# A decoder layer: signs dealt anew over the columns of a recurrence, and the last attention group in another order

## The chip, the cores and the metric

One core of one Trainium2 chip. The time is device microseconds from launch to the end of the program. Engines have one in-order queue each: TensorE (PE) multiplies and transposes, VectorE (DVE) and ScalarE (ACT) work element by element, GpSimd (POOL) masks, SyncE (SP) issues DMAs. They meet only through semaphores.

## The reference, cut to what matters

Two sequences of 1024 tokens, 256 wide, all in float32, go through three sublayers, each followed by a layer norm.

```
x = layernorm(x + gated_linear_attention(x))     # 16 heads, dk = 8, dv = 16
x = layernorm(x + cross_attention(x, ctx, idx))  # every token attends to 64 indexed rows out of 64
x = layernorm(x + transformer_block(x))          # causal attention, then a mixture of 8 experts, top 2
```

The gated attention is a recurrence over time: the state of each head is multiplied by a decay and gains the product of a key and a value; a query reads it out; then an RMS norm per head, a gate and a projection. The cross attention picks its 64 context rows by an integer index, with repeats, so its softmax can be computed from how often each of the 64 rows is named: the kernel counts. In the transformer block every token gets a causal attention, an output projection `a = o @ Wo + bo + x`, a layer norm of `a`, routing logits, a softmax over the best two of 8 experts, and those experts' two-layer GELU networks.

## The kernel before, in words

The kernel is written out engine by engine; `nc.Block()` opens a stage with one list of instructions per engine, and all engines meet between stages. A step is released with `then_inc` on a semaphore and awaited by name with `wait_ge`. There is no planner: the order on each engine is the order in the source. Four stages: the front (`front`, to about 212 us of the profile), the cross attention (`cross_blocks`, to 358), the causal attention (`attend`, to 632) and the experts (`moe`).

**The recurrence, in `front`.** The 256 value columns are worked on as 32 columns `jj` (`NJ`), 16 for each sequence, each an array of 128 partitions by 1024 steps. For each column VectorE runs three instructions: `product(jj)` (L521, value times key, in PSUM to `qh`), `state(jj)` (L526, the scan with the decay), `output(jj)` (L531, times the query). Its loop is `state(jj); product(jj + 1); output(jj)`, followed by a side job at some columns. TensorE spreads the values of column `jj + 2` (`values`, L307) two columns ahead, and after each four columns sums over the key dimension (`sums(q)`, L314) and transposes (`turn(q)`, L320). ScalarE copies between the two (`sums_out`, L685) and after them (`tokens`, L688). `qh` has six buffers, so `product(jj)` also waits for the `sums` of the columns that used its buffer.

Side jobs woven into the loop, by their VectorE step: `parts_lo(n)` (L514) makes the low half of a value group after ScalarE's `parts_hi(n)` (L680); `x_lo(k)` (L505) does so for an input block after ScalarE's `x_hi(k)` (L650); `log_sigmoid(1)` (L511); and the RMS norm of the first two blocks of tokens: `out_square(m)` on ScalarE (L830), `out_means(m)` on VectorE (L834), `out_root(m)` on ScalarE (L838), `out_gated(m)` on VectorE (L843 to L847), `out_turn(m)` on TensorE (L114), `out_copy(m)` on ScalarE (L855), and the projection. Both blocks use the same buffer `z` for `og[m]`: `out_square(1)` writes it after `out_copy(0)`, which waits for `out_turn(0)`, which waits for `out_gated(0)`.

**The signs.** To count indices, ScalarE makes 65 arrays `sign(2 * index + bias)` (`signs`, L695) into a ring of six, `RS`; TensorE adds four at a time into two banks (`counts(u)`, L335 and L337). `taken` says how many signs ScalarE has made by the end of each column. `count_at[u]` is the column at which TensorE runs `counts(u)`, the first by whose start the four are due; the sign `n` waits for `counts((n - 6) // 4)`. In each column the signs stand behind ScalarE's other steps.

**The last group, in `attend`.** The attention goes in 8 groups of 4 heads. In each, 10 quads of up to four PSUM banks of scores are made (`quad_scores(k)` in the last group, L1828 to L1834), ScalarE takes their exponentials (`last_exps(k)`, L2024), GpSimd masks the diagonal ones (`triangle`, L1671), and TensorE sums the values with them (`quad_sums`, L1857). Scores of a quad reuse the banks of the quad before it, so they wait for its exponentials. Into the last group the first block's way from attention output to routing weights is woven: `turn_sums`, `divide`, `turn_rows` and copies, `project` (L122, 16 matmuls), `residual` and `means` (L2276 to L2288), `deviation` on ScalarE (the root, L2240), `normed` (L2292, L2296), `turn_normed` (L114), `normed_copy` on ScalarE (L2244) and `rows_hi` on VectorE, `logits` (L2225), `best_two`, `exps`, `weights`. The exponential and the root have different activation tables. `warm(n, bank)` (L1864) issues n matmuls whose result nobody reads.

**The start of `moe`.** TensorE transposes the biases `eb` into bank 0 (L2479), waits for ScalarE's copy of them to `x_bias` (L2524), then starts the first layer of the first expert in banks 0 and 1 (L2439), whose GELU is L2522. ScalarE makes high parts of weights (L2189) from the buffers `x_raw`, VectorE low parts (L2194), after which SP refills `x_raw`. The routing steps of the later blocks use banks 6 and 7 (`RB`).

## Time and profile before

| | us |
|---|---|
| median of 3 runs | 1396.2 (1394.47 to 1398.4) |
| the profiled execution | 1390.58 |
| its span, first to last instruction | 1388.9 |
| TensorE busy | 1291.1, 93% |
| VectorE busy | 978.2, 70% |
| ScalarE busy | 646.8, 47% |
| GpSimd busy | 138.9, 10% |
| mean granted TensorE clock | 0.979 of full speed |

The busy shares are means over four stages that have different limits, so each stage has to be read by itself. An idle time is written in brackets behind the instruction that ended it, with what it waited for.

### The profile page before, as it was taken

The page shows a single profiled execution, that of the slowest core. Times are in us where ns is not written, and L with a number is a line of the kernel's source. Part 1 is how long each engine was busy: PE and PEld are TensorE (multiplying, and loading weights), DVE is VectorE, ACT ScalarE, POOL GpSimd, SP SyncE. Part 2 cuts the span into 40 slices and gives each one's busy share as a digit, 9 for nine tenths or more (in the row PEclk, how much of TensorE's full clock was granted, in tenths as well). Part 3 has the DMA queues.
Part 4 walks back from the last instruction along what each step waited for, and adds up shares of the span by engine and source line. Part 5 has one row for each costly group of instructions (what it writes and reads, how often), then busy time and mean ns, then how long its engine had stood idle before and what let it go on. Part 6 is the DMA issues. An engine that isn't in the chain of part 4 may idle for free.

```text
span 1388.9 us, 18750 instructions
## 1 busy us (share of the span) xinstructions
PE 1291.1 (93%) x7469; PEld 954.1 (69%) x7469; DVE 978.2 (70%) x1409; ACT 646.8 (47%) x946; POOL 138.9 (10%) x217
## 2 busy tenths in 40 slices
PE   8786768999889999999999999999999999999997
PEld 6353437666655555556888888888888888888886
DVE  7998996798788888856666656655655555556566
ACT  5697564436457877775323323232323223233233
POOL 5000002000513433211000000000000000000000
PEclk9998889999989999999999999999999999999999
DMA  4000001002722221213000012110201102010001
GB/s 137 1 1 0 0 1 35 0 1 71 211 82 58 63 61 51 66 31 107 2 15 17 0 36 71 46 39 16 68 16 39 46 16 68 16 38 16 1 16 46
DMA packets 38599, 55.76 MB, mean 40 GB/s; under 512 B 8976, under 2 KB 23744, under 8 KB 38512
## 3 DMA queue, kind: packets, MB, share of 16 engines
q1 hardware_dynamic: 33328, 43.67, 10.6%
q0 software_dynamic: 3648, 10.09, 2.5%
q8 instruction: 59, 0.97, 0.3%
q10 hardware_dynamic: 1536, 0.81, 0.2%
q14 instruction: 28, 0.23, 0.1%
HBM read 43.73 MB, written 10.55 MB: 39 GB/s over the span
## 4 chain that ended last, share of the span: by engine, by line
PE 50%; DVE 3%; ACT 1%; issue 0%; DMA 0%; ACTq 0%; DVEq 0%
PE PS L2439 24%; PE PS L2452 23%; PE PS L122 1%; PE PS L114 0%; PE PS L2465 0%; DMA x_raw<-L_ffn_e_w 0%; PE PS L2225 0%; DVE OT_all L2596 0%; DVE r_st L2279 0%; DVE r_on L2296 0%; DVE x_mid L2589 0%; DVE x_mid L2587 0%; DVE r_on L2276 0%; PE PS L2477 0%; PE PS L2203 0%
## 5 line engine op out<-in xcount | busy, mean ns | idle before, releaser
L2522 ACT ACTIVATE x_g<-PS,x_bias 128x512 f32<-128x512 f32 x256 | 175.8, 687 | 486.8 <-PE PS L2439 486.7
L2439 PE MATMUL PS<-x_h,x_w 128*128 128x512 f32 x1536 | 400.7, 396 | 0.3 <-ACT x_bias L2524 0.3
L2452 PE MATMUL PS<-x_mid,x_w 128*128 128x512 f32 x1488 | 383.8, 393 | 0.0
L2439 PEld LDWEIGHTS PS<-x_h,x_w 128*128 128x128 f32 x1536 | 287.0, 188 | 65.6 <-ACT x_bias L2524 0.5
L2452 PEld LDWEIGHTS PS<-x_mid,x_w 128*128 128x128 f32 x1488 | 279.3, 188 | 64.4
L2587 DVE CAST x_mid<-x_g 128x512 fp32r<-128x512 f32 x256 | 109.2, 427 | 270.0 <-ACT x_g L2522 270.0
L2065 DVE TENSOR_REDUCE a_M<-PS 128x2 f32<-128x1024 f32 (+1 forms) x144 | 170.6, 1222 | 24.0 <-PE PS L1780 17.4
L2589 DVE TENSOR_TENSOR x_mid<-x_g,x_mid 128x512 fp32r<-128x512 f32 x256 | 177.3, 693 | 8.8
L2003 ACT ACTIVATE f_parts<-PS 128x512 f32<-128x512 f32 x224 | 121.1, 599 | 34.7 <-PE PS L1834 28.4
L1857 PE MATMUL PS<-f_parts,aV 128*32 128x256 f32 (+1 forms) x960 | 74.7, 392 | 0.0
L695 ACT ACTIVATE c_hot<-c_idxT,c_cid 128x1024 bf16<-128x1024 bf16 x65 | 70.2, 1139 | 7.5 <-PE PS L335 7.5
L526 DVE TENSOR_TENSOR_SCAN qh<-decay,qh 128x1024 f32<-128x1024 f32 x32 | 73.0, 2281 | 0.0
L2419 POOL DMA_DIRECT2D x_wb<-route_w x31 | 16.7, 539 | 475.9 <-DVE OT_all L2596 453.3
L1834 PE MATMUL PS<-aQ,aK 64*128 64x512 f32 x192 | 51.7, 495 | 2.8 <-ACT V L2024 2.0
L307 PE MATMUL PS<-vparts,g_sel 128*128 128x512 f32 x128 | 40.4, 441 | 12.9 <-DVE qh L521 11.3
L1834 PEld LDWEIGHTS PS<-aQ,aK 64*128 64x128 f32 x192 | 20.3, 186 | 42.9 <-ACT f_parts L2003 27.9
L2596 DVE SCALAR_TENSOR_TENSOR OT_all<-PS,x_bias,x_wb 128x512 f32<-128x512 f32 x62 | 46.2, 745 | 0.0
L1776 PE MATMUL PS<-aK,aQ 64*128 64x512 f32 (+3 forms) x256 | 37.2, 341 | 9.5 <-DVE a_M L2065 6.8
L1671 POOL TENSOR_SCALAR_AFFINE_SELECT f_parts<-f_parts 128x512 f32<-128x512 f32 x45 | 28.6, 636 | 166.3 <-ACT f_parts L2003 142.4
L2194 DVE TENSOR_TENSOR x_w<-x_raw,x_w 128x1024 fp32r<-128x1024 f32 x32 | 39.1, 1228 | 4.0 <-ACT x_w L2189 4.0
L307 PEld LDWEIGHTS PS<-vparts,g_sel 128*128 128x128 f32 x128 | 23.6, 202 | 25.0 <-DVE qh L521 15.6
L521 DVE TENSOR_TENSOR qh<-PS,KT 128x1024 f32<-128x1024 f32 x32 | 38.5, 1203 | 1.4 <-PE PS L314 1.3
(371 smaller groups left out, 1599.2 us busy)
## 6 DMA issues: line engine op xcount, KB each, us to landing
x_raw<-L_ffn_e_w SPq DMA_DIRECT2D x32, 512.0 KB, 3.7
qk_parts<-f_parts SPq DMA_DIRECT2D x16, 512.0 KB, 3.9
x_wb<-route_w POOLq DMA_DIRECT2D x31, 256.0 KB, 3.4
aK<-qk_parts SPq DMA_DIRECT2D x96, 64.0 KB, 2.7
aQ<-qk_parts SPq DMA_DIRECT2D x96, 64.0 KB, 2.5
X<-x SPq DMA_DIRECT2D x4, 512.0 KB, 7.4
out<-X SPq DMA_DIRECT2D x3, 512.0 KB, 2.9
O<-itok_BxSx SPq DMA_DIRECT2D x2, 256.0 KB, 7.8
```

The costliest lines, as they stand in the source:

```text
L307: last = e.matmul(PS[:, 2 * (jj % 2) + half, :], self.sel[:, j, :], vparts[:, u, n % 2, half * BLK:(half + 1) * BLK], start=u == 0, stop=u ...
L526: e.tensor_tensor_scan(qh[:, jj % RQ, :], decay[:, batch(jj // HD)], qh[:, jj % RQ, :], 0.0, ALU.mult, ALU.add).then_inc(s_h, 1)
L695: e.activation(hot[:, n % RS, :], self.idxT[:, :], ACT.Sign, bias=self.cid[:, c:c + 1], scale=2.0).then_inc(s_sg, 1)
L1834: last = e.matmul(bank, K[q][R, s, tile(TB * h if kind == "k0" else kind)], Q[q][R, s, q0:q0 + BLK], start=True, stop=True)
L1857: last = e.matmul(PS[32 * j:32 * j + 32, 7, dst:dst + w], Vs[m % 2][:, kt, j, :], x, start=k in (0, 3) and half == 0, stop=k in (2, NQD - ...
L2003: e.activation(buf[k][:, j, :], PS[:, 4 + b % 3, :], ACT.Exp).then_inc(A.sem, 1)
L2065: e.tensor_reduce(dst, src, AX.X, ALU.max, negate=True).then_inc(VC.sem, 1)
L2439: last = e.matmul(PS[:, f % 2, :], w1[n % 2][u][:, kt, f * P:(f + 1) * P], self.rows(v, k)[:, kt, :], start=m == 0 and kt == 0, stop=m == ...
L2452: last = e.matmul(PS[:, 2 + 2 * (it % 2) + d, :], w2[n % 2][v][:, f, d * P:(d + 1) * P], mid[u][:, f % RM, :], start=f == 0 and m == 0, st ...
L2522: e.activation(g[s % RG][:, :], PS[:, f % 2, :], ACT.Gelu, bias=b1[:, n, f:f + 1]).then_inc(A.sem, 1)
L2587: e.tensor_copy(mid[0][:, f % RM, :], g[s % RG][:, :]).then_inc(V.sem, 1)
L2589: e.tensor_tensor(mid[1][:, f % RM, :], g[s % RG][:, :], mid[0][:, f % RM, :].bitcast(F32), ALU.subtract).then_inc(V.sem, 1)
```

## The change

In `front`: `taken` is dealt anew. By the end of columns 0 to 15 it was 0, 1, 2, 4, 6, 9, 12, 14, 16, 18, 21, 23, 25, 28, 30, 33; it becomes 0, 1, 3, 6, 9, 14, 16, 17, 18, 19, 20, 22, 24, 27, 29, 32, then 33, 35, 37, ... 47 for columns 16 to 23, 50, and the old values from column 25 on. At each fourth column one sign moves between `sums_out` and `tokens`. VectorE's side jobs move: most by half a column, from behind `output(jj)` to behind `state(jj + 1)`; `out_gated(0)` from column 18 to behind `output(19)`, straight before `out_means(1)`; `out_gated(1)` from behind `output(20)` to behind `output(21)`.

In the last group: the projection is in two pieces of eight matmuls with `quad_scores(5)` between them; the two `warm(2)` before the projection and before `turn_normed` go, and two `warm(2)` come around the last `quad_sums`; TensorE runs sums 3 and 4 ahead of scores 6 and 7; `logits` goes behind `quad_sums(7)`, ScalarE's root behind `last_exps(6)`.

In `moe`: the biases are transposed into the first of the banks `RB`, and TensorE does not wait for their copy.

```diff
-        taken = list(itertools.accumulate((0, 1, 1, 2, 2, 3, 3, 2, 2, 2, 3, 2, 2, 3, 2, 3, *[2] * (HD - 1), 1)))
+        taken = list(itertools.accumulate((0, 1, 2, 3, 3, 5, 2, 1, 1, 1, 1, 2, 2, 3, 2, 3, 1, 2, 2, 2, 2, 2, 2, 2, 3, 3, 2, 2, 2, 2, 2, 1)))
...
                     state(jj)
-                    if jj == 23:
+                    if jj == 2:
+                        parts_lo(1)
+                    elif jj == 6:
+                        x_lo(3, 4)
+                    elif jj == 11:
+                        log_sigmoid(1)
+                    elif jj == 12:
+                        parts_lo(2)
+                    elif jj == 18:
+                        self.out_means(e, 0)
+                    elif jj == 19:
+                        parts_lo(3)
+                    elif jj == 23:
                         self.out_rstd(e, 0)
...
                     output(jj)
-                    if jj == 1:
-                        parts_lo(1)
-                    elif jj == 3:
+                    if jj == 3:
                         x_lo(2, 4)
-                    elif jj == 5:
-                        x_lo(3, 4)
-                    elif jj == 10:
-                        log_sigmoid(1)
-                    elif jj == 11:
-                        parts_lo(2)
-                    elif jj == 17:
-                        self.out_means(e, 0)
-                    elif jj == 18:
-                        parts_lo(3)
+                    elif jj == 19:
                         self.out_gated(e, 0)
-                    elif jj == 19:
                         self.out_means(e, 1)
-                    elif jj == 20:
+                    elif jj == 21:
                         self.out_gated(e, 1)
...
                         sums_out(jj // 4 - 1)
+
+                        signs(range(taken[jj - 1], taken[jj - 1] + 1))
                         tokens(jj // 4 - 1)
...
-                    signs(range(taken[jj - 1] if jj else 0, taken[jj]))
+                    signs(range(taken[jj - 1] + (jj % 4 == 0) if jj else 0, taken[jj]))
...
                 quad_sums(NG - 1, 2)
-                warm(2, SPARE)
-                self.project(e, 0, FREE)
-                for k in range(5, 8):
+                self.project(e, 0, FREE, range(2))
+                quad_scores(5)
+                self.project(e, 0, FREE, range(2, TB))
+                for k in range(6, 8):
+                    quad_sums(NG - 1, k - 3)
                     quad_scores(k)
-                    quad_sums(NG - 1, k - 2)
-                warm(2, SPARE)
+                quad_sums(NG - 1, 5)
+                quad_sums(NG - 1, 6)
                 self.turn_normed(e, 0, FREE)
-                quad_sums(NG - 1, 6)
                 quad_scores(8)
+                quad_sums(NG - 1, 7)
                 self.logits(e, 0, FREE)
-                quad_sums(NG - 1, 7)
                 quad_scores(9)
                 quad_sums(NG - 1, 8)
+                warm(2, SPARE)
                 quad_sums(NG - 1, 9)
+                warm(2, SPARE)
...
                 last_exps(5)
+                last_exps(6)
                 self.deviation(e, 0)
-                last_exps(6)
...
-                e.transpose(PS[:, 0, 0:E * (NF + KD)], self.eb[:, :], self.ident[0:E * (NF + KD), 0:E * (NF + KD)]).then_inc(SM.sem, 1)
-                e.wait_ge(A.sem, A.at("b1"))
+                e.transpose(PS[:, RB[0], 0:E * (NF + KD)], self.eb[:, :], self.ident[0:E * (NF + KD), 0:E * (NF + KD)]).then_inc(SM.sem, 1)
```

## Rows read from the trace of the kernel before

**Rows 1.** Windows, two stretches: busy us (instructions) by engine, clock, DMA, GB/s.

```profile
24.00:200.00 176.00, 129.57 (x729) 80.48 (x728) 165.15 (x136) 120.94 (x128) 0.00 (x0) 0.89 0.00 1
590.00:632.80 42.80, 37.33 (x334) 22.02 (x330) 22.70 (x49) 31.05 (x56) 8.36 (x12) 0.96 0.09 26
```

**Rows 2.** Timeline, VectorE, recurrence: start, us, instruction, [idle before it, released by].

```profile
35.89 1.22 DVE L514 TENSOR_TENSOR vparts<-PS,vparts 128x1024 fp32r<-128x1024 f32 x1 [1.85 <-ACT vparts L680]
...
56.72 1.23 DVE L505 TENSOR_TENSOR XTp<-PS,XTp 128x1024 fp32r<-128x1024 f32 x1 [0.68 <-ACT XTp L650]
...
87.36 1.22 DVE L514 TENSOR_TENSOR vparts<-PS,vparts 128x1024 fp32r<-128x1024 f32 x1 [1.48 <-ACT vparts L680]
...
117.42 1.22 DVE L834 TENSOR_REDUCE go_ms<-z 128x64 f32<-128x1024 f32 x1 [2.15 <-ACT z L830]
...
139.29 0.55 DVE L843 RECIPROCAL go_rs<-go_rs 128x64 f32<-128x64 f32 x1 [1.97 <-ACT go_rs L838]
...
193.23 2.48 DVE L601 TENSOR_TENSOR c_Kblk<-PS,c_m 128x512 f32<-128x512 f32 x4 [0.43 <-PE PS L465]
...
200.52 0.69 DVE L984 CAST vparts<-PS 128x512 fp32r<-128x512 f32 x1 [0.69 <-PE PS L114]
```

**Rows 3.** Timeline, VectorE: one scan and the product behind it.

```profile
142.28 2.28 DVE L526 TENSOR_TENSOR_SCAN qh<-decay,qh 128x1024 f32<-128x1024 f32 x1
144.48 1.20 DVE L521 TENSOR_TENSOR qh<-PS,KT 128x1024 f32<-128x1024 f32 x1
```

**Rows 4.** Timelines of VectorE, TensorE, ScalarE: from `out_gated(0)` to `out_square(1)`.

```profile
126.07 1.23 DVE L847 TENSOR_TENSOR z<-z,G 128x1024 f32<-128x1024 f32 x1
...
127.44 1.94 PE L114 MATMUL PS<-ident,z 128*128 128x128 f32 x8 [4.24 <-DVE z L847]
...
129.42 1.02 ACT L855 ACTIVATE QT<-PS 128x1024 f32<-128x1024 f32 x1 [3.15 <-PE PS L114]
130.34 1.05 ACT L830 ACTIVATE z<-O 128x1024 f32<-128x1024 f32 x1
```

**Rows 5.** Timeline, ScalarE, recurrence: a gate copy, `tokens(0)`, the two signs of column 28.

```profile
40.34 1.03 ACT L675 ACTIVATE G<-PS 128x1024 f32<-128x1024 f32 x1 [3.45 <-PE PS L283]
...
52.69 1.05 ACT L688 ACTIVATE O<-PS 128x512 f32<-128x512 f32 x1 [1.18 <-PE PS L320]
...
188.97 2.16 ACT L695 ACTIVATE c_hot<-c_idxT,c_cid 128x1024 bf16<-128x1024 bf16 x2
```

**Rows 6.** Timeline, TensorE, last group: projection, scores 5, logits.

```profile
607.79 3.61 PE L122 MATMUL PS<-r_Wo,r_onT 128*128 128x256 f32 x16
611.33 0.73 PE L1834 MATMUL PS<-aQ,aK 64*128 64x512 f32 x4
...
625.31 1.95 PE L2225 MATMUL PS<-r_Wr,r_onT 128*128 128x8 f32 x16
```

**Rows 7.** Timeline, ScalarE, last group: exponentials 5, root's table, exponentials 6, 8.

```profile
611.93 2.06 ACT L2024 ACTIVATE V<-PS 128x512 f32<-128x512 f32 x4 [2.81 <-PE PS L1834]
614.01 1.28 ACT L2240 ACT_TABLE_LOAD   x1
...
616.92 2.07 ACT L2024 ACTIVATE V<-PS 128x512 f32<-128x512 f32 x4
...
625.19 2.06 ACT L2024 ACTIVATE f_parts<-PS 128x512 f32<-128x512 f32 x4 [0.71 <-PE PS L1829]
```

**Rows 8.** Windows, TensorE alone: busy (instructions), granted clock, DMA, GB/s.

```profile
604.00:608.00 4.00, 4.00 (x39) 1.00 0.01 2
...
616.00:618.00 2.00, 0.43 (x1) 1.00 0.00 0
...
620.00:622.00 2.00, 2.00 (x15) 0.50 0.00 0
```

**Rows 9.** Timeline, TensorE: the first layer's first six matmuls in `moe`.

```profile
633.43 2.87 PE L2439 MATMUL PS<-x_h,x_w 128*128 128x512 f32 x6 [0.33 <-ACT x_bias L2524]
```

**Rows 10.** The chain that ended last, in order of time: start, us, what.

```profile
645.48 5.29 DMA x_raw<-L_ffn_e_w
```

More of the change, by code:

```diff
@@ L2209, in turn_rows, with project @@
         self.transposes(e, self.on, 0, rb).then_inc(self.SR.sem, 1)
-    def project(self, e, m, rb):
-        e.wait_ge(self.VR.sem, self.VR.at("onT0", m))
-        e.wait_ge(self.AR.sem, self.AR.at("onT1", m))
-        self.token_major(e, self.onT, self.Wo, rb).then_inc(self.SR.sem, 1)
+    def project(self, e, m, rb, ts=range(TB)):
+        if 0 in ts:
+            e.wait_ge(self.VR.sem, self.VR.at("onT0", m))
+            e.wait_ge(self.AR.sem, self.AR.at("onT1", m))
+        last = self.token_major(e, self.onT, self.Wo, rb, ts)
+        if TB - 1 in ts:
+            last.then_inc(self.SR.sem, 1)
     def turn_normed(self, e, m, rb):
@@ L2523, in _ @@
                 e.wait_ge(SM.sem, SM.at("b1"))
-                e.activation(bias[:, :], PS[:, 0, 0:E * (NF + KD)], ACT.Copy).then_inc(A.sem, 1)
+                e.activation(bias[:, :], PS[:, RB[0], 0:E * (NF + KD)], ACT.Copy).then_inc(A.sem, 1)
                 for q in range(2, 4):
```

## The prediction

> **What bounds the kernel now.** I read the windows by stage first, then the timeline of the engine that is fullest in each changed stage, then the chain of waits. In the recurrence, 24 to 200 us, VectorE is busy 165.2 of 176 us and no other engine is as full [rows 1]. So the time of this stage is VectorE's work plus its stalls, and the reader is to look for the brackets: 1.85 and 1.48 before two `parts_lo`, 0.68 before `x_lo(3)`, 2.15 before `out_means(0)`, 1.97 before `out_gated(1)`, 0.43 before the key blocks, 0.69 at the stage's end [rows 2]. The last group, up to 632.8, is different: TensorE is busy 37.3 of 42.8, ScalarE 31.1, VectorE 22.7 [rows 1], so a loop through several engines sets its end: scores on TensorE, exponentials on ScalarE, and once each the root and the normed rows. There the reader is to see ScalarE idle 2.81 us for scores 5, which stood behind the whole projection [rows 6, 7]. In `moe` TensorE is nearly full, so what comes before it is passed on whole: the stages are separated by a meeting of all engines, and no transfer that started in an earlier stage is late in the next.
>
> **The recurrence.** The work of VectorE is the same, instruction for instruction; only stalls change. Removed are 1.85 + 0.68 + 1.48 + 2.15 + 1.97 = 8.1 us [rows 2], if each awaited step is now done in time. One scan, 2.20 us from start to start [rows 3], goes between.
> - `parts_lo(1)`: VectorE was free at 34.0, one scan later it is 36.2, and ScalarE's high part was there at 35.9. No stall.
> - `x_lo(2)` is not moved, but gets early. Behind 36.2 come `parts_lo(1)` and four multiplications at 1.12 each and a scan: 44.0. ScalarE's gate copy, at 40.34 before [rows 5], follows `parts_lo(1)` and starts at 40.6; then two signs instead of one, at 1.08 each (2.16 for two [rows 5]), and `x_hi(2)`, 1.0: 44.8. A new stall, 0.8.
> - `x_lo(3)`: its high part was ready at 56.7 [rows 2]. It now comes 1.15 earlier by what is gained so far, but sign 6 stands before `tokens(0)` and waits for `counts(0)`, which TensorE runs behind its turn: 1.0 for the counts and 1.1 for the sign, so 57.6. VectorE is there at 57.0. New stall 0.6. At the other fourth columns the sign placed there is not held up, and fits into the 1.18 us that ScalarE idles before `tokens` [rows 5]; it costs nothing and takes 1.08 off what stood behind.
> - `parts_lo(2)` is wanted at 86.6 and ready at 85.2: fewer signs in columns 7 to 10 bring ScalarE's steps forward.
> - `out_means(0)` is wanted at 114.45. The copy before the square moves up with ScalarE and the square ends near 113.7: no stall. `parts_lo(3)` is wanted at 120.04, ready at 119.97; cover is gone if ScalarE is 0.1 later, and costs what it is late.
> - `out_means(1)` is the price. It now follows `out_gated(0)` directly, and waits for `out_square(1)`, which writes the same buffer and so waits for that very gate. Before, the gate ended at 127.3 (126.07 + 1.23) and the square at 131.4 (130.34 + 1.05) [rows 4]: transposes 1.94 at the low clock, copy, square and the hand-overs, 4.1 us. Before, column 19's scan and multiplications lay beside it. Now nothing does: a new stall of 4.1. Queued behind it on VectorE is the state of column 20, and all that follows.
> - `out_gated(1)` comes a column and a half later than the root it waited 1.97 for: free. Its own work is 142.28 - 139.29 = 3.0 us [rows 2, 3], unchanged.
>
> In the loop 8.1 - 0.8 - 0.6 - 4.1 = 2.6 us go; a stalled instruction also loses the 0.08 by which the next else overlaps [rows 3], two stalls fewer, 0.2: 2.8. At the end, the sign in the gap before `tokens(6)` frees ScalarE 0.8 sooner for the copies of the context keys, whose follower stalled 0.43, and for the last six signs, on which TensorE's last counts and transposes hang, which stalled VectorE 0.69 [rows 2]. I take 0.7 of the 1.1. The stall before `product(30)` depends on the second block's norm and stays. Sum: 3.5 us. Bounds: no gain but the tail's (0.7), if `parts_lo(3)`, `x_lo` and `out_means(1)` eat the rest; and 4.5, if the transposes run at the full clock and the x stalls vanish.
>
> **The last group.** TensorE is through with sums 2 at 607.2. Half of the projection (3.61 / 2 [rows 6]) brings it to 609.0, where scores 5 begin instead of at 611.33. ScalarE starts 0.60 behind them (611.93 - 611.33 [rows 6, 7]): 609.6, 2.3 earlier; its table, buffers and the copy before it are ready. The second half ends at 611.5 and the residual starts as before. The mean and variance are there at 614.7 as before. Sums 3 (1.07 us) then stand before scores 6, so ScalarE's exponentials 6 run 613.1 to 615.1. The root with its two table loads takes 614.01 to 616.92, 2.9 us [rows 7]; it now runs 615.1 to 618.0, and exponentials 7 end at 620.1. That is only 0.8 ahead of before (620.9). The normed rows are ready at 618.35, 1.0 later than before, but TensorE turns them at once, being through with sums 5 and 6 at 617.3, and not behind scores 7, a sum and a warm-up. So the copy of them follows exponentials 7 directly (620.1, 0.8 us) and exponentials 8 run from 620.9 instead of 625.19 [rows 7]: 4.3 earlier. Behind these: sums 7 wait for the mask (620.8) and end at 621.9, logits 1.95 us [rows 6] to 623.8, scores 9, exponentials 9 from 624.4 to 625.5 (before 628.8), mask, sums 9, copy, as before. The end of the stage keeps the 4.3 to 4.4. The warm-ups around sums 9 lie beside the mask and the last copy and cost nothing, within 0.2. I take 4.3. Upper bound 5; lower 2.5, if TensorE is at half clock from 618.4 on: then turn, scores 8, sums 7 and logits take 1.8 us more.
>
> **The start of `moe`.** TensorE no longer idles 0.33 [rows 9]. But the first GELU is followed by weights that ScalarE takes from `x_raw`, and the chain goes through the landing of these (5.29 us [rows 10]); they are issued by work that starts at the copy of the biases, which does not move. So most of it is lost there. I take 0.1; bounds 0 and 1.1: at the full clock the six matmuls would take 1.4 instead of 2.87 [rows 9].
>
> **Sum.** 3.5 + 4.3 + 0.1 = 7.9 us. The profiled execution took 1390.58, so its like would take 1382.7. The median of the runs is 5.6 above that execution, and I take the difference off it: 1396.2 - 7.9 = 1388.3.
>
> **Rivals.** A measurement of this kernel can tell about 0.3%, 4.2 us, from no change.
> - A, the clock takes part of the last group. After 616 to 618 with TensorE busy 0.43 of 2 us, the granted clock was 0.50 in 620 to 622, the 1.2 GHz level [rows 8]. The new order still has a wait of about 1.0 at 617.3, and two warm-ups are gone. The group then gives 2.5: total 6.1, 1390.1. For it: the wait. Against: it is half as long, and before it TensorE works from 607 on.
> - B, the recurrence gives only its tail: the stall at `out_means(1)` grows or `parts_lo(3)` is late. Total 0.7 + 4.3 = 5.0: 1391.2. For it: the margin of 0.07 us.
> - C, what is gained in the last group is hidden anyway: if the weights for `moe`, or the low clock at its start, set the pace, the gain there is absorbed. About 3.5 at most is left: 1392.7, and with B, 1395.5. Against: the first weights landed long before, and later loads are issued by work of the stage itself.
> - D, slower. The warm-up at 607.2 and the next were what kept TensorE at 2.4 GHz; without them it falls to 1.2 GHz from the projection on. About 17 us of TensorE's work lie from there to the end of the group, nearly all on its path. Each us of it at the low level costs another; past 7.8 us of it, the whole gain is gone. With all 17: 17 - 7.8 = 9 slower, 1405; with 12: 1400. Against: TensorE hardly pauses there; four us before, also full of transposes, have clock 1.00 [rows 8].
>
> The Trainium skill, "TensorE: Matmul & The Clock Gate", Part 4: PE-mode transpose, says that transposes do not count as TensorE activity for the clock in the same way as matmuls. It would speak for A and D, since two warm-ups leave a stretch with turns in it. By that rule D's time would be 1400 to 1405. The window 604 to 608, a quarter of it transposes, has the full clock, so the trace does not bear the rule out here.
>
> **Chances.** Forecast 0.62, A 0.15, B 0.08, C 0.10, D 0.05. The forecast's own range is 1386 to 1391. The range to hold 8 in 10 takes in A and B, the upper bounds of the terms (1396.2 - 4.5 - 5 - 1.1 = 1385.6), and about 1.5 us of scatter in a median: 1384.5 to 1393.5. Faster by over 0.3%, below 1392.0: forecast, A, most of B, 0.82. Within 0.3%: C and the rest of B, 0.13. Slower: D, 0.05.
>
> **What would show it.** Right: VectorE's bracket before `out_means(1)` near 4.1 and none before `out_means(0)`, `out_gated(1)` and the `parts_lo`; brackets of 0.8 and 0.6 before `x_lo`; the second stage 3.5 earlier; exponentials 5 at 2.3 earlier and 8 at 4.3 earlier against the group's start; TensorE's clock 1.00 in the group. Wrong: a clock below 1 between 607 and 618 (D) or after it (A), a `parts_lo(3)` with a stall over 1 us (B), or a new wait for `x_raw` in `moe` as long as what was gained (C).

## The result, and the profile after

| | before | after |
|---|---|---|
| median, us | 1396.45 (6 runs, 1391.48 to 1398.4) | 1388.34 (6 runs, 1382.51 to 1391.79) |
| ratio | | 0.9941, 95% interval 0.9918 to 0.9964 |
| the profiled execution | 1390.58 | 1391.79 |
| its span | 1388.9 | 1390.1 |
| its mean granted TensorE clock | 0.979 | 0.975 |

The change takes 0.6% off, and the interval excludes both no change and the 0.3% that a measurement can just tell. 1388.3 had been forecast. Twelve kernels were measured later, in three groups of four, each group beside the kernel before on one chip; the changed kernel, measured again among them, had 1388.40 and a ratio of 0.9951 (0.9931 to 0.997).

But the two profiled executions say the opposite: after is 1.2 us longer than before. That of before was shorter than all six times in its median, that of after was the longest of its six. The first thing to look at is the clock. The changed kernel was profiled a second time ("after, again"): there its span was 1381.6 us at a mean granted clock of 0.983, and the first time 1390.1 us at 0.975. 8.5 us lie between two executions of one program. Over all 68 later runs of the kernel before, the time falls by about 0.93 us for each 0.001 of mean granted clock; over those of the changed kernel by 1.1 to 1.2. So below, a kernel has two figures: its ratio to before, and its time at equal clock, read off a line through its own runs at clock 0.979 (their scatter about the line is 0.4 to 1.2 us). By the line before has 1390.9 and after 1387.2: 3.7 us less. The rest of the 8.1 goes with the median clock, 0.975 before and 0.9785 after. The line is an aid to reading and no price: where a kernel has more of the full clock because its path has changed, the reading at equal clock takes that part from the change. It is also uncertain: the lines of single kernels, of 6 to 12 runs, have slopes from 0.5 to 1.5 us per 0.001, and 0.979 is the upper end of what before ever had. With one slope for all kernels, 0.97, the readings are 1390.8 for before and 1387.3 for after, so these two stand; where another reading hangs on the slope, both are given below.

The shares of the changed kernel (page, first part: busy us, share, instructions) show no less work. VectorE and ScalarE are as busy as they were, and TensorE is busy longer, because part of its work ran slower:

```profile
PE 1296.3 (93%) x7469; PEld 958.2 (69%) x7469; DVE 977.2 (70%) x1409; ACT 647.5 (47%) x946; POOL 139.2 (10%) x217
```

**The recurrence after.** VectorE's stalls of the loop and its tail, timeline of the changed kernel:

```profile
46.48 1.23 DVE L505 TENSOR_TENSOR XTp<-PS,XTp 128x1024 fp32r<-128x1024 f32 x1 [2.06 <-ACT XTp L650]
60.57 1.22 DVE L505 TENSOR_TENSOR XTp<-PS,XTp 128x1024 fp32r<-128x1024 f32 x1 [1.78 <-ACT XTp L650]
89.91 1.23 DVE L514 TENSOR_TENSOR vparts<-PS,vparts 128x1024 fp32r<-128x1024 f32 x1 [0.28 <-ACT vparts L680]
118.35 1.22 DVE L836 TENSOR_REDUCE go_ms<-z 128x64 f32<-128x1024 f32 x1 [0.51 <-ACT z L832]
134.61 1.22 DVE L836 TENSOR_REDUCE go_ms<-z 128x64 f32<-128x1024 f32 x1 [4.13 <-ACT z L832]
...
192.33 1.23 DVE L521 TENSOR_TENSOR qh<-PS,KT 128x1024 f32<-128x1024 f32 x1 [1.17 <-PE PS L307]
...
202.42 0.69 DVE L986 CAST vparts<-PS 128x512 fp32r<-128x512 f32 x1 [0.82 <-PE PS L114]
```

As [rows 2] are read, the brackets of 1.85 and 1.97 are gone, 1.48 has become 0.28 and 2.15 has become 0.51. In their place stand 4.13 before `out_means(1)` and 2.06 and 1.78 before the two `x_lo`. Together 8.8 us, where 8.1 had stood: in this execution the loop gained nothing. A wait of 1.17 before the last product is new beside them. TensorE's work ahead of that product ran at the low clock: the eight transposes of `turn` took 1.97 us, and in the second execution 1.09, without the wait.

```profile
187.62 1.97 PE L320 MATMUL PS<-ident,OT 128*128 128x128 f32 x8 [1.14 <-ACT OT L685]
```

The second execution of the same program:

```profile
45.33 1.22 DVE L505 TENSOR_TENSOR XTp<-PS,XTp 128x1024 fp32r<-128x1024 f32 x1 [0.57 <-ACT XTp L650]
121.50 1.23 DVE L514 TENSOR_TENSOR vparts<-PS,vparts 128x1024 fp32r<-128x1024 f32 x1 [1.50 <-ACT vparts L680]
132.09 1.22 DVE L836 TENSOR_REDUCE go_ms<-z 128x64 f32<-128x1024 f32 x1 [4.12 <-ACT z L832]
...
197.79 0.69 DVE L986 CAST vparts<-PS 128x512 fp32r<-128x512 f32 x1 [0.45 <-PE PS L114]
```

Here only 6.2 us of stall are left in the loop, and the stage is through 4.6 us sooner. The 4.12 does not vary; the others do. The transposes inside the 4.12 stand behind a long pause of TensorE, and took 1.94 us in all 14 profiles. For the others, look at TensorE's gate matmuls, which ScalarE and then `x_lo(2)` wait for. In the first execution, then in the second:

```profile
37.77 4.63 PE L283 MATMUL PS<-Wgp,XTp 128*128 128x256 f32 x24 [1.77 <-DVE vparts L514]
```

```profile
38.11 3.14 PE L283 MATMUL PS<-Wgp,XTp 128*128 128x256 f32 x24 [1.77 <-DVE vparts L514]
```

The same 24 matmuls after the same wait of 1.77 us take 1.5 us more, and the stall of `x_lo(2)` is 1.5 longer. Over 24 to 212 us the granted clock was 0.88 in the first and 0.91 in the second (before: 0.90).

**The last group after**, where it ran at full clock, that is in the second execution. TensorE, with line 1836 the scores of quad 5, 114 the turn of the normed rows, 1859 sums 9, 1866 the second warm-up, 2487 the first matmul of `moe`:

```profile
606.65 0.73 PE L1836 MATMUL PS<-aQ,aK 64*128 64x512 f32 x4
...
616.19 1.09 PE L114 MATMUL PS<-ident,r_on 128*128 128x128 f32 x8 [0.88 <-DVE r_on L2304]
...
623.96 0.64 PE L1859 MATMUL PS<-f_h,aV 128*32 128x256 f32 x8 [0.26 <-POOL f_h L1673]
624.52 0.73 PE L1866 MATMUL PS<-a_idr 128*128 128x512 f32 x2
626.17 0.26 PE L2487 MATMUL PS<-ident,r_eb 80*128 80x80 f32 x1 [0.91 <-PEq L1636]
```

and ScalarE beside it (exponentials 5, the root's table, exponentials 8):

```profile
607.25 2.06 ACT L2029 ACTIVATE V<-PS 128x512 f32<-128x512 f32 x4 [0.63 <-PE PS L1836]
...
612.91 1.28 ACT L2248 ACT_TABLE_LOAD   x1
...
618.40 2.09 ACT L2029 ACTIVATE f_parts<-PS 128x512 f32<-128x512 f32 x4
```

The group's first scores began at 588.28 here and at 590.76 before. From there: scores 5 come 18.37 us in, where it was 20.57 (611.33, [rows 6]); exponentials 8 come 30.12 in, where it was 34.43 (625.19, [rows 7]); the group takes 37.89, where it took 42.08. The 2.81 us of ScalarE's idling [rows 7] is 0.63. TensorE's windows have clock 1.00 throughout (busy, instructions, clock, DMA share, GB/s):

```profile
590.00:600.00 10.00, 9.59 (x97) 1.00 0.32 96
600.00:612.00 12.00, 12.00 (x106) 1.00 0.03 11
612.00:626.00 14.00, 11.91 (x116) 1.00 0.00 1
```

In the execution of after that was profiled first, the group took 40.12 us, and TensorE was at its 1.2 GHz level twice:

```profile
598.00:600.00 2.00, 2.00 (x16) 0.51 0.00 0
600.00:602.00 2.00, 2.00 (x24) 0.64 0.03 8
...
628.00:630.00 2.00, 2.00 (x18) 0.69 0.00 0
630.00:632.00 2.00, 2.00 (x14) 0.50 0.04 8
```

**The start of `moe`.** Its first six matmuls took 1.62 us instead of 2.87 [rows 9], but the gain is mostly waited away: TensorE, the changed kernel.

```profile
634.39 0.26 PE L2487 MATMUL PS<-ident,r_eb 80*128 80x80 f32 x1 [1.01 <-PEq L1636]
634.54 1.62 PE L2447 MATMUL PS<-x_h,x_w 128*128 128x512 f32 x6
...
638.88 3.00 PE L2447 MATMUL PS<-x_h,x_w 128*128 128x512 f32 x12 [0.88 <-ACT x_g L2529]
```

ScalarE still waits for the landing of `x_raw`, in the second execution:

```profile
632.43 1.06 ACT L2194 ACTIVATE x_w<-x_raw 128x1024 fp32r<-128x1024 f32 x1 [0.80 <-DMA x_raw<-L_ffn_e_w]
```

From the first matmul of `moe` to that of the kernel's last group of matmuls it is 742.24 us before, 741.89 and 741.64 in the two executions of after. Over all profiles this length is 741.49 to 742.24 with the old start (five, mean 741.91) and 741.25 to 742.37 with the new one (nine, mean 741.82).

### The profile page after: what moved, and what is told of

Read it like the earlier page. It is cut to its first block, busy times and chain, and to the rows that moved or that the text cites. A ratio compares the mean times of both kernels' runs of the same rounds, so it can differ in the third digit from the quotient of the medians.

```text
span 1390.1 us, 18750 instructions
## 1 busy us (share of the span) xinstructions
PE 1296.3 (93%) x7469; PEld 958.2 (69%) x7469; DVE 977.2 (70%) x1409; ACT 647.5 (47%) x946; POOL 139.2 (10%) x217
## 4 chain that ended last, share of the span: by engine, by line
PE 50%; DVE 3%; DMA 1%; issue 0%; ACT 0%; ACTq 0%; DVEq 0%
PE PS L2447 24%; PE PS L2460 23%; PE PS L122 1%; DMA x_raw<-L_ffn_e_w 1%; PE PS L114 0%; PE PS L2473 0%; PE PS L2233 0%; DVE x_w L2199 0%; DVE OT_all L2603 0%; DVE r_st L2287 0%; DVE r_on L2304 0%; DVE x_mid L2596 0%; DVE x_mid L2594 0%; DVE r_on L2284 0%; PE PS L2485 0%
## 5 line engine op out<-in xcount | busy, mean ns | idle before, releaser
L307 PEld LDWEIGHTS PS<-vparts,g_sel 128*128 128x128 f32 x128 | 24.5, 209 | 21.4 <-DVE qh L521 10.5
```

Of the source, the lines that this page charges most:

```text
L307: last = e.matmul(PS[:, 2 * (jj % 2) + half, :], self.sel[:, j, :], vparts[:, u, n % 2, half * BLK:(half + 1) * BLK], start=u == 0, stop=u ...
```

## The experiments

Each is a kernel of its own. "At clock 0.979" is the reading described above. Each ratio is to runs of before on the same chip; experiments 1 to 4, 5 to 8 and 9 to 12 had one chip each, so medians are compared only within these groups.

**1 to 3: the parts alone, and the whole again.** Front only: the new `taken` and VectorE's new order, nothing else.

```diff
-        taken = list(itertools.accumulate((0, 1, 1, 2, 2, 3, 3, 2, 2, ...
+        taken = list(itertools.accumulate((0, 1, 2, 3, 3, 5, 2, 1, 1, ...
...
                     state(jj)
+                    if jj == 2:
+                        parts_lo(1)
```

> The change of the front stage alone (signs and VectorE order), last group and experts as before. Theory 1 (each part brings its own stalls' worth, as forecast): VectorE's idle time in the recurrence falls by 2.6 to 3.5 us and the median by 3.5, ratio 0.9975. Theory 2 (the one profile of after read literally: the front stage ends 1.9 us later than before): the median rises by about 2, ratio 1.0014, and the whole gain of the change comes from elsewhere. A profile with new stalls of 0.8 and 0.6 before the two x_lo speaks for 1, one with about 2 each for 2.

Last group only:

```diff
-                self.project(e, 0, FREE)
+                self.project(e, 0, FREE, range(2))
+                quad_scores(5)
+                self.project(e, 0, FREE, range(2, TB))
...
-                self.deviation(e, 0)
                 last_exps(6)
+                self.deviation(e, 0)
```

> The new order of the last attention group alone. Theory 1: the group ends 4.3 us earlier, ratio 0.9969; from the first scores of the group to the first matmul of the experts 37.8 us instead of 42.1. Theory 2 (as the one profile of after shows, where this stretch took 40.1): 2.0 earlier, ratio 0.9986, because TensorE ran at the low clock at the end of the group and the two matmuls put before sums 9 then delay them.

The changed kernel again, with no edit:

> The changed kernel unchanged, for a second profile and more times. Theory 1 (the change is worth about 8 us, and the first profile was taken in an execution with more low clock): ratio 0.994, and at a mean clock of 0.978 or more the profile shows the front stage ending earlier than 212.4 us, as the kernel before does. Theory 2 (front stage slower by itself): the front ends after 213.5 again.

| | median us | ratio (95%) | at clock 0.979 |
|---|---|---|---|
| front only | 1392.58 | 0.9986 (0.9974, 0.9998) | 1388.3 |
| last group only | 1390.89 | 0.9978 (0.9964, 0.9993) | 1389.3 |
| after, again | 1388.40 | 0.9951 (0.9931, 0.997) | 1387.2 |

The front is worth 2.0 us by its ratio (0.3 to 3.6) and 2.6 at equal clock (1.6 with the common slope), the last group 3.1 (1.0 to 5.0) and 1.6 (1.8). The last group's own length, first scores to the first matmul of `moe`: 40.13 with the last group only, 43.86 with the front only, both with stretches at the low clock, against 37.89 (after, again) and 42.08 (before). Like is to be compared with like here. In six of the 14 profiles TensorE's clock fell some five us into the group, before anything that the change moves, and the steps behind it came 1.0 later. Without this fall the old order takes 42.08 to 42.24 (four profiles) and the new one 37.89 to 37.98 (four): 4.2 less. With it, the old order takes 43.86 (one) and the new one, as in the changed kernel, 40.12 to 40.16 (three): 3.7 less. With the group's old order the clock fell behind TensorE's pause before the turn, as in [rows 8]; windows of the front only:

```profile
620.00:622.00 2.00, 2.00 (x8) 0.50 0.00 0
```

The front's stalls in its own profile (VectorE from 24 to 204 us: who waited for whom, us in total, times, longest):

```profile
DVE go_ms L836 <- ACT z L832: 4.5, 2, 4.1
...
DVE XTp L505 <- ACT XTp L650: 1.3, 2, 0.7
...
DVE vparts L514 <- ACT vparts L680: 0.9, 2, 0.6
```

The `x_lo` stalls add to 1.3, near the forecast's 0.8 and 0.6, and the means stand for 4.1.

**4: the forecast's price taken back.** `out_means(1)` goes one column later, so that the scan and the multiplications of column 20 lie beside the transposes, the copy and the square.

```diff
                     elif jj == 19:
                         self.out_gated(e, 0)
+                    elif jj == 20:
                         self.out_means(e, 1)
```

> The changed kernel with the means of the second block (out_means(1)) one column later, behind output(20). In after VectorE idles 4.1 us for the square that this step needs, directly behind the gate that the square waits for. Theory 1: that stall is a pure loss; with a column of 4.45 us between, it goes whole and the root and gate of block 1 are still in time: 4 us faster than after, ratio to before 0.991. Rival: the root, which stands on ScalarE behind tokens(4), is then late, the gate behind output(21) stalls 1 to 2 us, or product(22) waits for sums(4): 1 to 2 us are left of the 4.

Measured: 1382.34 (1377.85 to 1387.31), ratio 0.9915 (0.9892 to 0.9938); at clock 0.979, 1383.1. Its stalls (VectorE, as above):

```profile
DVE XTp L505 <- ACT XTp L651: 1.3, 2, 0.8
...
DVE go_ms L837 <- ACT z L833: 0.6, 1, 0.6
```

The 4.1 is gone and nothing took its place; the 0.6 is that before `out_means(0)`. In medians the kernel is 6.1 us faster than the changed one beside it, by the ratios 5.0, at equal clock 4.1, the stall itself. It does not rest on this one kernel: the four with this edit (4, 5, 6, 12) read 1382.7 to 1383.5 at equal clock, and the changed kernel and its two neighbours without it (10, 11) 1386.9 to 1387.2. The kernel has the lowest median of all, and beats both kernels.

**5: without the warm-ups around sums 9**, on top of experiment 4.

```diff
-                warm(2, SPARE)
                 quad_sums(NG - 1, 9)
-                warm(2, SPARE)
```

> r4_means_later without the four warm-up matmuls around sums 9. In two of three profiles with the new group TensorE was at the low clock there, and the two before sums 9 then delayed them by 0.9 us. Theory 1 (the warm-ups cost where the clock is low and buy nothing, since the first GELU of the experts waits for weights from x_raw anyway): 0.5 us faster than r4_means_later in the median, and the first matmuls of the experts may be at the low clock without moving anything behind them. Theory 2 (they keep the clock up into the experts, which counts): 1 to 1.5 us slower than r4_means_later, the first six matmuls of the experts in 2.9 instead of 1.6 us and their end passed on.

Measured: 1383.41, ratio 0.9911 (0.9894 to 0.9929), at clock 0.979 1382.7. Not to be told from experiment 4. The clock fell at the logits in its profile too (the sums behind them took 1.93 us, the 1.2 GHz level), and the warm-ups then no longer stood before sums 9.

**6: `x_lo(2)` half a column later**, on top of experiment 4.

```diff
                     state(jj)
+                    elif jj == 4:
+                        x_lo(2, 4)
...
-                    if jj == 3:
-                        x_lo(2, 4)
```

> r4_means_later with x_lo(2) behind state(4) instead of behind output(3), a scan later. Theory 1: its stall (0.6 to 0.8 us with TensorE at the full clock before it, 2.06 with the low clock) goes wholly or to 0, and nothing else is late: 0.7 us faster than r4_means_later at the full clock, up to 2 at the low one, and less scatter. Rival: sums(0) wait for this step on TensorE, so turn(0), the sign and x_lo(3) get 1 to 2 us later: the stall moves there and the sum is 0.

Measured: 1385.15, ratio 0.9926 (0.9904 to 0.9949), at clock 0.979 1383.5: no gain. The stall moved:

```profile
58.79 1.23 DVE L505 TENSOR_TENSOR XTp<-PS,XTp 128x1024 fp32r<-128x1024 f32 x1 [2.62 <-ACT XTp L651]
```

`x_lo(2)` has no bracket any more, and `x_lo(3)` has 2.62. TensorE's `sums(0)` start only behind `x_lo(2)`, and the whole way from there to `x_lo(3)` hangs on them: from one `x_lo` to the other it is 12.7 us here and 13.1 in experiment 4, so a later `x_lo(2)` makes `x_lo(3)` late. The 2.62 is not to be set against the 0.57 and 0.75 of experiment 4, whose gate matmuls took 3.14 us. Here they took 4.63, as in the first profile of after, where the two brackets add to 3.8.

**7 and 8: the front's two parts apart.** Signs only: the new `taken` and the sign before `tokens`, VectorE's order as before. Order only: the opposite.

```diff
+                        signs(range(taken[jj - 1], taken[jj - 1] + 1))
                         tokens(jj // 4 - 1)
```

> The kernel before with the new deal of signs alone; VectorE's order, last group and experts as before. Theory 1 (signs make ScalarE's steps of columns 7 to 19 earlier, and VectorE's order turns that into fewer stalls; alone each is worth little): without the order, the waits for parts_lo(1) (1.85) and gated(1) (1.97) stay, x_lo(2) and x_lo(3) gain 1 to 2 us of stall, parts_lo(2) and means(0) lose 1 to 2: within 1 us of before. Theory 2 (the deal is the part that pays): 2 us faster.

```diff
                     state(jj)
+                    elif jj == 18:
+                        self.out_means(e, 0)
...
+                    elif jj == 19:
+                        self.out_gated(e, 0)
+                        self.out_means(e, 1)
```

> The kernel before with VectorE's new order of side jobs alone, old deal of signs. Theory 1: the stalls before parts_lo(1), x_lo(3), parts_lo(2) and gated(1) go (6.0 us), means(0) loses most of its 2.15, the 4.1 before means(1) comes, parts_lo(3) may be 1 to 3 late: 2 to 3 us faster than before, so the order is what pays in the front. Theory 2 (the order needs the signs): ScalarE is late at parts_lo(2), means(0) and parts_lo(3), within 1 us of before.

| | median us | ratio (95%) | at clock 0.979 |
|---|---|---|---|
| signs only | 1391.18 | 0.9976 (0.9956, 0.9997) | 1389.7 |
| order only | 1395.47 | 1.0005 (0.9993, 1.0017) | 1393.7 |

The signs alone save 3.3 us (0.4 to 6.1), the order alone none. At equal clock it would cost 2.8 by its own line, whose slope of 0.5 is the flattest of all, and 1.2 with the common slope; by its ratio it is between 1.0 better and 2.4 worse. The stalls with the signs alone:

```profile
DVE vparts L514 <- ACT vparts L680: 1.8, 1, 1.8
DVE XTp L505 <- ACT XTp L650: 1.3, 1, 1.3
...
DVE go_rs L844 <- ACT go_rs L839: 0.9, 1, 0.9
```

Of the five brackets in [rows 2], those before `out_means(0)` and `parts_lo(2)` have gone with nothing moved on VectorE, and 1.97 is 0.9. (This profile had a clock of 0.94 over 24 to 212 us, the others 0.86 to 0.91.) With the order alone:

```profile
DVE go_ms L834 <- ACT z L830: 5.4, 2, 4.1
DVE z L511 <- ACT decay L666: 2.0, 1, 2.0
...
DVE vparts L514 <- ACT vparts L680: 1.5, 1, 1.5
DVE XTp L505 <- ACT XTp L650: 1.3, 1, 1.3
```

the 4.1 is there, and a 2.0 before `log_sigmoid(1)`, which before's profile has not; but experiment 2, with nothing moved in the front, had 1.3 there.

**9: `moe` only.** ScalarE's copy of the biases reads the new bank too.

```diff
-                e.transpose(PS[:, 0, 0:E * (NF + KD)], ...
-                e.wait_ge(A.sem, A.at("b1"))
+                e.transpose(PS[:, RB[0], 0:E * (NF + KD)], ...
```

> The kernel before with the new start of the experts alone (biases transposed into another bank, TensorE not waiting for their copy). Theory 1: the stage is set by the landing of x_raw, so of the 0.33 us 0.1 to 0.35 are left: not to be told from no change in the median; in the profile, from the bias transpose to the last matmul group 741.9 us instead of 742.2. Theory 2 (more, if the low clock at the stage's start is shortened as well): 1 us.

Measured: 1394.62, ratio 0.9991 (0.9981 to 1.0001), at clock 0.979 1391.1 (before 1390.9). The rest of the kernel behind the transposes took 741.92 in its profile, 742.24 before. That is 0.3 less, within what such a length varies by.

**10: the two removed warm-ups back**, in the changed kernel.

```diff
                 quad_sums(NG - 1, 2)
+                warm(2, SPARE)
                 self.project(e, 0, FREE, range(2))
...
                 quad_sums(NG - 1, 6)
+                warm(2, SPARE)
                 self.turn_normed(e, 0, FREE)
```

> The changed kernel with the two removed warm-up pairs back, ahead of the projection and ahead of turn_normed. Theory 1 (the clock does not need them there): the first pair adds its 0.6 to 0.7 us to the chain, as scores 5 stand behind it, the second lies in the wait for the normed rows and costs 0: 0.6 us slower than the changed kernel. Theory 2 (rival D of the prediction, without them the clock falls in the group): 2 us faster than the changed kernel, with the share of the low clock smaller in the group.

Measured: 1390.59, ratio 0.9960 (0.9943 to 0.9977); at clock 0.979, 1386.9 against 1387.2. By the ratios 1.3 us slower than after, again, within the intervals, at equal clock the same; this is not settled. What it does show: in this execution the warm-ups did not hold the clock. The second pair ran at 620.56, and behind it TensorE's windows show:

```profile
624.00:626.00 2.00, 2.00 (x26) 1.00 0.00 0
626.00:628.00 2.00, 2.00 (x17) 0.67 0.00 0
628.00:630.00 2.00, 2.00 (x17) 0.50 0.04 8
```

**11: the changed kernel with VectorE's old order.**

```diff
                     output(jj)
+                    if jj == 1:
+                        parts_lo(1)
...
-                        self.out_means(e, 1)
-                    elif jj == 21:
+                    elif jj == 19:
+                        self.out_means(e, 1)
+                    elif jj == 20:
                         self.out_gated(e, 1)
```

> The changed kernel with VectorE's order of before in the recurrence: new signs, new last group, new start of the experts. Signs alone gave 3.8 us, the order alone nothing, both 2.6. Theory 1 (with the new signs, the order costs more by its 4.1 us before means(1) than it saves at parts_lo(1), x_lo(3) and gated(1)): 0 to 2 us faster than the changed kernel, ratio to before 0.993 to 0.994. Theory 2 (the parts add as single medians say only by chance; at an equal clock both together were 1.4 us better than signs alone): 1 to 1.5 us slower than the changed kernel.

Measured: 1385.92 (8 runs, 1380.58 to 1393.16), ratio 0.9943 (0.9921 to 0.9966), at clock 0.979 1387.2, as after. So the order brought nothing that can be measured, also when all the rest is there. It may pay once its 4.1 is removed: experiment 4, which differs from this kernel in VectorE's order alone, reads 1383.1 at equal clock, but by the ratios, 0.9915 and 0.9943, the two are not clear of each other. The profile has one stall of 4.8 us in the place of the 4.1 (VectorE, 24 to 204 us):

```profile
DVE XTp L505 <- ACT XTp L650: 4.8, 1, 4.8
```

It belongs to this execution: the same front had 1.3 there in experiment 7. TensorE, ahead of it, was at the low clock here (transposes 1.97 us, there 1.09):

```profile
52.37 1.97 PE L320 MATMUL PS<-ident,OT 128*128 128x128 f32 x8 [1.14 <-ACT OT L685]
```

**12: sign 6 behind `tokens(0)`**, on top of experiment 4.

```diff
                         sums_out(jj // 4 - 1)
-                        signs(range(taken[jj - 1], taken[jj - 1] + 1))
+                        if jj > 4:
+                            signs(range(taken[jj - 1], taken[jj - 1] + 1))
                         tokens(jj // 4 - 1)
...
-                    signs(range(taken[jj - 1] + (jj % 4 == 0) if jj else 0, taken[jj]))
+                    signs(range(taken[jj - 1] + (jj > 4 and jj % 4 == 0) if jj else 0, taken[jj]))
```

> r4_means_later with sign 6 behind tokens(0) instead of before. There it waits for counts(0), which TensorE runs behind its turn, and holds tokens(0) and with it x_hi(3). Theory 1: tokens(0) comes 2 to 4 us earlier, the stall before x_lo(3) (0.75 us in r4_means_later's profile, 1.8 in after's) goes, 0.7 to 1.5 us faster than r4_means_later. Rival: the three signs then stand before x_hi(3), or x_hi(3) waits for TensorE's transposes all the same: no change.

Measured: 1383.78, ratio 0.9910 (0.9893 to 0.9927), at clock 0.979 1383.2: as experiment 4. ScalarE in its profile:

```profile
53.85 1.05 ACT L689 ACTIVATE O<-PS 128x512 f32<-128x512 f32 x1 [2.06 <-PE PS L320]
55.69 3.23 ACT L696 ACTIVATE c_hot<-c_idxT,c_cid 128x1024 bf16<-128x1024 bf16 x3 [0.78 <-PE PS L337]
```

`tokens(0)` went first, and then the signs waited for `counts(0)` all the same. The bracket before `x_lo(3)` is 0.74. In experiment 4 it was 0.75, but there TensorE's transposes ahead of it took 1.09 us, and here 1.97. The first profile of after had 1.97 too, and a bracket of 1.78; against it ScalarE's `x_hi(3)` now starts at 58.82 instead of 59.53. So where the clock is low the edit may save up to 1 us; the times do not show it.

## Why the prediction was right, and where its steps were not

**The sum.** 7.9 us forecast, 8.1 by the first medians, 6.8 by the ratio of the second set (4.2 to 9.6). The first is the forecast; the second lies between it and A. That the median came within 0.1 us of 1388.3 is luck: the single times of after lie 9.3 us apart. Added up by the lengths of the stages, the parts make 4.2 + 2.6 + 0.1 = 6.9; by the ratios of the parts alone it is 2.0 + 3.1 + 1.3 = 6.4, the 1.3 of `moe` being not clear of nothing; read at equal clock the whole makes 3.7. These don't agree, and what of the 8.1 is path and what clock stays open.

**The last group, 4.3: right.** Scores 5 2.2 us earlier (forecast 2.3), exponentials 8 4.3 earlier (4.3), the group 4.2 shorter (4.3), where the clock stayed up in its first part and again behind the logits. Rival C did not happen: `moe` keeps its length, so what the group gains is passed on. The steps between hold too: the root followed exponentials 6 with two table loads at 1.28, and the turn waited 0.88 (about 1.0 forecast).

Rival A is a part of the truth. In the first profile the low clock took 1.0 at 598 to 602, before anything that the change moves, and the rest at the end. The group is 2.0 shorter there than in before's profile, near A's 2.5, but that one had no early fall; against the old order with such a fall, experiment 1, it is 3.7 shorter. And A's place was wrong: the clock was 1.00 around the wait at the turn (616 to 626 in both profiles of after), and fell from the logits on.

"The warm-ups around sums 9 cost nothing" failed where the clock is low. At full clock the mask ended the wait before sums 9 (0.26, the row at 623.96). In the first profile sums 9 started at 632.06, directly behind the warm-up; by the distance between the exponentials 9 and their mask in the second execution (623.96 less 622.11, 1.85) it could have started at 631.05. That is 1.0 us, outside the 0.2 that was given.

**The recurrence, 3.5: probably too large, and credited to the wrong edit.** The front alone gives 2.0 by ratio and 2.6 at equal clock; 3.5 is at the edge of the ratio's interval (0.3 to 3.6), so it is not excluded. The next stage's first matmul starts at 209.8, 211.9, 212.2 and 214.5 in the four profiles with the changed front (after twice, 1, 10), and at 212.6, 214.1 and 217.5 in the three with the old one (before, 2, 9): the means are 2.6 apart, and single profiles of one front up to 4.9. The brackets before side jobs in the loop add to 8.8, 6.2, 6.6 and 6.5 with the changed front, and to 8.1, 8.6 and 10.5 with the old one: 2.0 less in the mean, where 2.6 had been forecast.
- The step that holds best is the new stall at `out_means(1)`: 4.1 forecast, 4.12 and 4.13 measured, and its removal brought 4.1 at equal clock.
- The steps for `x_lo(2)` and `x_lo(3)`, 0.8 and 0.6, hold at full clock (0.57 and 0.75 in experiment 4) and fail at low clock, 2.06 and 1.78. The forecast took TensorE's steps ahead of them from one execution, as if fixed.
- `parts_lo(3)`, wanted at 120.04 and ready at 119.97: this margin of 0.07 was used up in six of the eight profiles with the new signs and order, with stalls of 0.56 to 1.54 (1.50 in after, again). It is rival B's mechanism, at a part of B's price, and the forecast had it at nothing.
- The working counted 8.1 us of stalls as removed by signs and moves together. Experiments 7, 8 and 11 show what it never asked: what each would do alone. The signs alone save 3.3 by ratio, the order alone nothing: what it wins by its half columns it pays back with the 4.1 that it creates. Whether both together are better than the signs alone stays open: by the ratios the signs alone are ahead (3.3 to 2.0), within the intervals; at equal clock both are, by 1.4 with their own lines and by 0.5 with the common slope.

**`moe`, 0.1: right.** 0.1 shorter in the mean of nine profiles against five, within the scatter; the chain still goes through `x_raw`, as said. Alone it cannot be told from nothing.

**From one profile to a median.** The forecast took the median as its profiled execution plus 5.6 us, a constant. It is no constant, and most of it goes with the clock: that execution had 0.979 where the median of the later runs has 0.975, which is 3.7 us by the line. The changed kernel has a median clock of 0.9785, and by the line about half of the 8.1 us comes with that. No step of the forecast spoke of it. Why a kernel with shorter stalls gets more of the full clock is only argued here: TensorE pauses less. For it: with the 4.1 us stall taken away as well, the median clock is 0.9805; signs only, with 4.0 us of stalls in the loop in its profile, has 0.978, the whole front, with 6.6, has 0.975. Against: the changed kernel with VectorE's old order has 0.979, with 8.9 us of stalls in its profile.

**D and the rule on transposes.** Without the two warm-ups the stretch from the projection to the logits kept clock 1.00 in both profiles. D did not happen, and experiment 10 shows that with them the clock falls behind the logits all the same.
The Trainium skill, "TensorE: Matmul & The Clock Gate", Part 4: PE-mode transpose, says that transposes do not count for the clock as matmuls do. By this rule the turn of the normed rows and its surroundings should have been at risk. The trace shows no such harm here: eight transposes at 616.19 took 1.09 us, at the 2.4 GHz level, and the window around them, 612 to 626, has clock 1.00. Longer runs of transposes were not tried.

## What to carry to other kernels

Before two profiles are compared, compare their granted clocks: here a change that is 0.6% faster looked 0.1% slower in its own pair of profiles. A line of time over clock through the single runs gives a second reading, as good as its slope. Compare stretches with the same pattern of clock: the last group was 4.2 us shorter like for like, and 2.0 in the two profiles taken as they came. When a step is moved right behind the one that it depends on through other engines, the whole round trip becomes a stall (4.1 us here); one column of independent work between them gives it all back. And when an edit has two halves, work out each alone, since one of them may only be paying for the other.

## What the runs showed of the hardware

- Executions of one program on one core differ by 8 to 10 us (0.6 to 0.7%), most of it with the mean granted clock, about 1 us for each 0.001. The same wait of 1.77 us was followed by 24 matmuls in 4.63 us or in 3.14, and by these windows of TensorE, in the first profile of after:

```profile
38.00:40.00 2.00, 2.00 (x12) 0.56 0.00 0
40.00:42.00 2.00, 2.00 (x13) 0.58 0.00 0
```

  where the second has 1.00 in both.
- In the last group the clock fell behind the logits in five of the nine profiles with the new order (in the other four it stayed), though TensorE did not pause there: it ran the 16 matmuls of the logits. Timeline of TensorE, the first profile of after:

```profile
626.62 1.95 PE L2233 MATMUL PS<-r_Wr,r_onT 128*128 128x8 f32 x16
...
629.04 1.93 PE L1859 MATMUL PS<-f_parts,aV 128*32 128x384 f32 x16
```

  The sums at 629.04 take 1.07 us at full clock (after, again, at 621.96). The five are those in which the clock had also fallen early in the group; in the other four it was 1.00 there too. What decides it was not found.
- Behind TensorE's pause of 4.1 to 6.8 us for `out_gated(0)`, its eight transposes took 1.94 us in all 14 profiles, where eight such transposes take 1.09 at the full clock. They are a part of the stall of 4.1, which does not vary either.
- A change of activation table cost ScalarE its 1.28 us and nothing behind it: the load at 621.50 was followed by an exponential at 622.80, 1.30 later.
